# Time mix of an RWKV-style block: roots ahead of the mix's low halves, rows split ahead of the mix, the time row in the last bank, the first input in four transfers

## The reference, cut to what matters

```python
xn  = _layernorm(x)                       # the input of both branches
x1  = _ln(xn, ln1_g, ln1_b)
xln = _ln(x1, tm_g, tm_b)
xs  = _shift(xln)                         # one step later in time
mix = xln * time_first + xs * (1.0 - time_first)
v   = xln @ Wv
r   = sigmoid(mix @ Wr)
vmix = einsum('bth,th->bh', v, exp(time_decay * (T - 1 - t)))
x2  = xn + r * (vmix @ Wo + bo)
xc  = _ln(_ln(x2, ln2_g, ln2_b), cm_g, cm_b)
rc  = sigmoid(xc @ Wcr)                   # used later with relu(shift(xc) @ Wck)^2 @ Wcv
```

## Time and profile before

| | us |
|---|---|
| median of 3 runs | 1819.31 (1818.61 to 1824.56) |
| the profiled execution | 1819.79 |
| its span | 1818.2 |
| PE busy | 1671.1 (92%) |
| DVE busy | 1156.1 (64%) |
| ACT busy | 1032.1 (57%) |
| POOL busy | 507.7 (28%) |
| granted PE clock, mean | 0.98 |

### The profile page before, as it was taken

The page is one execution under the profiler, slowest core; times in us unless marked ns, Lnnn a source line. Parts: engine busy times, 40 slices in busy tenths (PEclk is TensorE's granted clock), DMA queues, the critical chain, the costliest instruction groups (busy, mean ns, idle before and its releaser), DMA issues.

```text
span 1818.2 us, 27152 instructions
## 1 busy us (share of the span) xinstructions
PE 1671.1 (92%) x9270; PEld 1424.0 (78%) x9270; DVE 1156.1 (64%) x2177; ACT 1032.1 (57%) x1809; POOL 507.7 (28%) x648
## 2 busy tenths in 40 slices
PE   2888899999999989999988999999999999999996
PEld 2666687877777777777776788989898898989895
DVE  6688632246787677687666776575666666666653
ACT  5466463334666666666764534565656565665652
POOL 3344310101122111222112031333334343433432
PEclk9899999999999999999999999999999999999998
DMA  5355657883356444575426445686767676767671
GB/s 193 115 169 189 194 181 197 249 238 91 104 171 140 113 130 120 136 202 131 110 79 170 108 152 188 211 276 204 265 214 254 227 246 227 251 226 259 223 245 24
DMA packets 114567, 328.21 MB, mean 181 GB/s; under 512 B 29615, under 2 KB 29615, under 8 KB 100722
## 3 DMA queue, kind: packets, MB, share of 16 engines
q1 hardware_dynamic: 94194, 287.42, 48.0%
q0 software_dynamic: 15696, 31.21, 9.5%
q10 hardware_dynamic: 4592, 8.52, 1.3%
HBM read 264.31 MB, written 68.94 MB: 183 GB/s over the span
## 4 chain that ended last, share of the span: by engine, by line
PE 59%; DVE 7%; ACT 6%; issue 4%; POOL 1%; DMA 1%; ACTq 0%; DVEq 0%; POOLq 0%
PE bank L53 17%; PE bank L55 17%; PE bank L54 17%; PE bank L2172 2%; DVE hd_a L1955 1%; PE bank L2158 1%; PE bank L2203 1%; DVE hd_masked L2014 1%; PE bank L2200 1%; DVE ex_w_lo L2608 1%; PE bank L2202 1%; ACT hd_a_hi L1823 1%; ACT hd_relu L1803 1%; PE bank L2711 1%; DVE hd_p_lo L2021 1%
## 5 line engine op out<-in xcount | busy, mean ns | idle before, releaser
L2608 DVE TENSOR_TENSOR ex_w_lo<-ex_stage,ex_w_hi 128x1024 fp32r<-128x1024 f32 x207 | 248.6, 1236 | 171.6 <-ACT ex_w_hi L2518 166.8
L1726 POOL TENSOR_SCALAR_AFFINE_SELECT hd_p_full<-hd_p_full 128x128 f32<-128x128 f32 (+1 forms) x192 | 93.0, 493 | 437.3 <-ACT hd_p_full L1853 434.5
L2444 POOL TENSOR_TENSOR ex_a_lo<-ex_a,ex_a_hi 128x256 fp32r<-128x256 f32 x128 | 92.6, 746 | 293.2 <-ACT ex_a_hi L2540 293.0
L53 PE MATMUL bank<-ex_x_hi_a,ex_w_hi 128*128 128x256 f32 x512 | 145.1, 283 | 0.4 <-DVE ex_a L2646 0.3
L53 PE MATMUL bank<-ex_x_hi_b,ex_w_hi 128*128 128x256 f32 x512 | 144.7, 283 | 0.0
L55 PE MATMUL bank<-ex_x_hi_b,ex_w_lo 128*128 128x256 f32 x512 | 144.3, 282 | 0.0
L54 PE MATMUL bank<-ex_x_lo_b,ex_w_hi 128*128 128x256 f32 x512 | 144.3, 282 | 0.0
L55 PE MATMUL bank<-ex_x_hi_a,ex_w_lo 128*128 128x256 f32 x512 | 144.2, 282 | 0.0
L54 PE MATMUL bank<-ex_x_lo_a,ex_w_hi 128*128 128x256 f32 x512 | 144.0, 281 | 0.0
L2515 ACT ACTIVATE ex_w_hi<-ex_stage 128x1024 fp32r<-128x1024 f32 x134 | 133.8, 1048 | 0.6 <-DMA ex_stage<-in_w_moe 0.6
L53 PE MATMUL bank<-ex_w_hi,ex_a_hi 128*128 128x512 f32 x312 | 126.2, 404 | 0.3 <-DVE ex_w_lo L2608 0.3
(11 more groups left out here) (321 smaller groups left out, 5000.9 us busy)
## 6 DMA issues: line engine op xcount, KB each, us to landing
ex_stage<-in_w_moe SPq DMA_DIRECT2D x69, 1536.0 KB, 6.9
first_w<-in_w_moe SPq DMA_DIRECT2D x23, 1536.0 KB, 6.8
st_qk<-scratch_qk SPq DMA_DIRECT2D x64, 256.0 KB, 3.7
st_raw<-in_w_up SPq DMA_DIRECT2D x64, 256.0 KB, 2.8
st_raw<-in_w_dn SPq DMA_DIRECT2D x64, 256.0 KB, 2.9
st_qk<-scratch_qk SPq DMA_DIRECT2D x128, 64.0 KB, 3.5
tm_x_in<-in_x SPq DMA_DIRECT2D x4, 1024.0 KB, 5.6
scratch_xn<-tm_xn SPq DMA_DIRECT2D x4, 1024.0 KB, 6.2
```

Of the source, the lines that this page charges most:

```text
L53: pe.matmul(out, lhsT=w_hi, rhs=x_hi, start=first, stop=False)
L1726: pool.affine_select(out=p_full[:, i % 2, at:at + blocks * P], in_=p_full[:, i % 2, at:at + blocks * P], compare_op=ALU.is_ge, fill=0.0, b ...
L2444: pool.tensor_tensor(a_lo[:, chunk.par, m, :], a[:, m, :], a_hi[:, chunk.par, m, :].bitcast(F32), ALU.subtract).then_inc(wide_lo_ready, 1)
L2608: return dve.tensor_tensor(dst, src, hi.bitcast(F32), ALU.subtract)
```

## The change

- POOL: the root for `x2(b)` and the roots for `x(b + 2)` now stand between `low_x(b + 1)` and `low_mix(b + 1)` of sequence b; `add_x2(b)` stands behind `low_mix(b + 1)`.
- `split_x`: ACT makes `xT` and `x_hi` of all four banks first (eight ops), and then the four parts of `mix` from `xT` in SBUF, with the scale `time_first` alone; the constants `tf_scale` fall away. `x_lo` waits for the two ops of its bank, `v` for two ops and one `x_lo` at a time, and frees bank m when it comes to it.
- `r` and `rc` wait for one low half at a time in their first row block (j = 0).
- The time row goes to bank 3; `turn_x(b + 1)` waits for the residual only ahead of its last bank. The same holds for `turn_xs(0)`.
- Start: `x_in` of batch 0 comes in four DMAs with a semaphore each, and the moments start on the first; the four centring ops stand ahead of the wait for the root; ACT makes `decay` ahead of `norm_x(0)`, splits weight 0 and 1 ahead of `norm_x1(0)`, each when its own DMA has landed, and weight 2 behind `high_mix(0)`; `inverse_roots_x(1)` follows `low_mix(0)` as before.

```diff
             def low_x(b):
-                low(x_lo, lambda c: xT[:, c, 1:S + 1], x_hi, x_split, b * 3 * HC, 3, x_lo_ready)
+                low(x_lo, lambda c: xT[:, c, 1:S + 1], x_hi, x_split, b * 3 * HC, 2, x_lo_ready)
...
-            def sequence(b, before, more):
-                if before:
-                    add_x2(b - 1)
-                    inverse_root(C, (b - 1) * STATS_C)
-                if more:
-                    inverse_roots_x(b + 1)
+            def sequence(b, before, more, more2):
                 if before:
                     inverse_root(C, (b - 1) * STATS_C + MOMENTS + AFFINE)
                 if more:
                     inverse_root(A, (b + 1) * STATS_A + FIRST + AFFINE)
-                if not more:
+                else:
                     root(0)
                 if before:
                     low_xc(b - 1, xcT)
                 if more:
                     low_x(b + 1)
+                inverse_root(C, b * STATS_C)
+                if more2:
+                    inverse_roots_x(b + 2)
+                if more:
                     low_mix(b + 1)
+                add_x2(b)
...
-                    act.activation(mix[:, c, :], psum[c][:, :], ACT.Identity, bias=tf_scale[:, 1, c:c + 1],
-                                   scale=tf_scale[:, 0, c:c + 1]).then_inc(x_split, 1)
+                act.wait_ge(x_split, b * 3 * HC + 2 * HC)
+                for c in range(HC):
+                    act.activation(mix[:, c, :], xT[:, c, 1:S + 1], ACT.Copy,
+                                   scale=vecs[:, V_TF, c:c + 1]).then_inc(x_split, 1)
...
-            norm_x(0)
             act.wait_ge(const_in, 16 * N_CONST)
...
+            norm_x(0, TT)
+            high_w(0)
+            high_w(1)
             norm_x1(0)
             act.wait_ge(consts_ready, CONSTS)
             split_x(0)
             high_mix(0)
+            high_w(2)
             sequence(0, False)
...
             first_moments_x(0, False)
-            first_scales_x(0)
             dve.wait_ge(const_in, 16 * N_CONST)
+            dve.wait_ge(stat[A], MOMENTS)
+            centred(A, t1, x_in, R_G1)
+            first_scales_x(0, TT)
...
-            norm_x1(0)
+            norm_x1(0, True)
...
-            def turn(src, bank, done):
+            def turn(src, bank, done, last_free=None):
                 for c in range(HC):
+                    if last_free and c == HC - 1:
+                        pe.wait_ge(*last_free)
...
                     for k in range(HC):
+                        if j == 0:
+                            pe.wait_ge(lo_ready, before + k + 1)
...
-                        if m == 0 and k == 0:
-                            pe.wait_ge(x_split, b * 3 * HC + 3 * HC)
+                        if k == 0:
+                            pe.wait_ge(x_split, b * 3 * HC + 2 * (m + 1))
...
-                    pe.matmul(psum[0][:, :], lhsT=vmix_wide[:, m, :], rhs=wo[:, m, :], start=(m == 0), stop=False)
+                    pe.matmul(psum[HC - 1][:, :], lhsT=vmix_wide[:, m, :], rhs=wo[:, m, :], start=(m == 0), stop=False)
...
-                pe.wait_ge(x2_step, b * 2 * TT + TT)
-                turn_x(b + 1)
+                turn_x(b + 1, True)
```

More of the change, by code:

```diff
@@ L153, in mix_project_phase @@
         const_in = sem("const_in")
-        w_in = sem("w_in")
+        w_in = [sem(f"w_in{n}") for n in range(3)]
         w_hi_ready = sem("w_hi_ready")
@@ L159, in mix_project_phase @@
         x_loaded = sem("x_loaded")
+        x0_loaded = [sem(f"x0_loaded{j}") for j in range(TT)]
         stat = {A: sem("stat_a"), C: sem("stat_c")}
@@ L211, in mix_project_phase @@
         N_CONST = 6
-        CONSTS = HC + 4
+        CONSTS = HC + 2
         R = TT + 1
@@ L247, in sequence @@
                     xc_halves_out(b - 1)
-            load_x(0)
+            for j in range(TT):
+                sp.dma_start(x_in[:, j, :], d["x"][0][j * P:(j + 1) * P, :]).then_inc(x0_loaded[j], 16)
             sp.dma_start(vecs[:, :, :], d["vecs"]).then_inc(const_in, 16)
@@ L409, in _ @@
             low_mix(0)
[L410 to L415, removed]
+            inverse_roots_x(1)
+            sequence(0, False, True, True)
+            with pool.Fori(1, B - 2) as b:
+                sequence(b, True, True, True)
+            sequence(B - 2, True, True, False)
+            sequence(B - 1, True, False, False)
             inverse_root(C, (B - 1) * STATS_C + MOMENTS + AFFINE)
@@ L432, in normed, with norm_x, high_w @@
                                    scale=rstd[:, chain, j:j + 1]).then_inc(ready, 1)
-            def norm_x(b):
-                normed(xn, x_in, A, b * STATS_A + FIRST, xn_ready)
+            def norm_x(b, first_halves=0):
+                normed(xn, x_in, A, b * STATS_A + FIRST + first_halves, xn_ready)
+            def high_w(n):
+                act.wait_ge(w_in[n], 16)
+                act.activation(w_hi[n][:, :, :].rearrange("p k n -> p (k n)"), w_stage[:, n, :],
+                               ACT.Copy).then_inc(w_hi_ready, 1)
             def norm_x1(b):
@@ L617, in scales, with centred @@
                 dve.wait_ge(stat[chain], end)
-            def affine_norm(chain, dst, src, row_g, row_b, at, root):
+            def centred(chain, dst, src, row_g):
                 for j in range(TT):
@@ L623, in affine_norm @@
                                              ALU.subtract, ALU.mult).then_inc(stat[chain], 1)
+            def affine_norm(chain, dst, src, row_g, row_b, at, root, begun=False):
+                if not begun:
+                    centred(chain, dst, src, row_g)
                 for j in range(TT):
@@ L801, in turn, with turn_x @@
                     t.then_inc(done, 1)
-            def turn_x(b):
+            def turn_x(b, before):
                 pe.wait_ge(norm_ready[A], b * TT + TT)
-                turn(t1, 0, x_turned)
+                turn(t1, 0, x_turned, (x2_step, (b - 1) * 2 * TT + TT) if before else None)
             def turn_xc(b):
@@ L833, in r @@
             def r(b):
-                pe.wait_ge(m_lo_ready, b * HC + HC)
-                by_token(1, m_hi, m_lo, r_done)
+                by_token(1, m_hi, m_lo, m_lo_ready, b * HC, r_done)
             def time_row(b):
@@ L840, in time_row @@
                 for m in range(HC):
[L841 to L842 removed]
+                    pe.matmul(psum[HC - 1][:, :], lhsT=vmix_wide[:, m, :], rhs=wo[:, m, :], start=(m == 0), stop=False)
+                pe.matmul(psum[HC - 1][:, :], lhsT=ones_row[:, :], rhs=bo_row[:, :], start=False,
                           stop=True).then_inc(r_done, 1)
             def rc(b):
[L846 to L847 removed]
+                by_token(2, xc_hi, xc_lo, xc_lo_ready, b * HC, rc_done)
             def sequence(b, before):
@@ L907, in _ @@
             pe.wait_ge(consts_ready, CONSTS)
-            turn_x(0)
+            turn_x(0, False)
             pe.wait_ge(w_lo_ready, 1)
```

38 lines of the change are left out of this document (15 added, 23 removed).

## The result

The changed kernel takes 1810.7 us (median of six runs, 1808.3 to 1816.9); the kernel before took 1824.4 in its six runs beside them (1818.6 to 1825.7). The ratio of the runs is 0.9941 with a 95% interval of 0.9925 to 0.9957: 10.8 us less (8 to 14), where 15.8 were forecast; the two medians lie 13.7 apart, at the edge of that interval. The sign is as forecast, the time is 0.7 outside the range. The profiled execution has a span of 1806.5 us instead of 1818.2.

What follows compares the result with a forecast made beforehand. TensorE was taken as the bound, its first-phase waits reaching the total whole. Terms 4.8 + 5.6 + 0.3 + 1.2 + 4.2 - 0.3 = 15.8 us off 1819.8 gave 1804.0, median 1803.5; range 1800 to 1810.

Steps and rivals of the forecast that it cites:

- The bound: TensorE sets the pace from the second phase on, so time taken out of the first phase comes out of the total whole.
- The start: Rows in at 12.2, turn_x(0) at 25.5 instead of 28.0, low_w(2) ending at 41.5 instead of 42.4.
- one of my signs of being wrong: Listed: low_w(2) ending after 42.4, idle ahead of L841, clock 0.50 beyond v's first block, new wait ahead of q(0)/second phase.
- The term of 0.9: At the start, DVE's path to batch 1 gains 0.9 us through low_w(2) ending sooner.
- turn_x(1): Its start leads by 4.8 us: 3.66 from the time row in bank 3, 0.3 from gate_r, 0.9 from the start.
- v(1): Starts 3.65 us after turn_x(1) instead of 9.24, gaining 5.6, for a lead of 10.4.
- the rival that small gaps hold the clock down: TensorE, fed by low halves, misses full clock in v(0), v(1), rc(2): 29 us lost, 1833 in all; chance 0.03.
- Batch 1: Roots' new place avoids a stall; waits of 0.90 and 0.30 go, those of 7.04 stay; lead 11.9.
- rc(2): With one wait for each xc_lo, rc(2) ends 3.8 to 4.4 us sooner, taken as 4.2.
- v_tokens(0): Comes close to q_lo and may wait: -0.3 us.
- the first rival: Part of the gain only, DVE ruling the path (late rows, slower beside POOL): lead 10, 1809 us; chance 0.2.

Runs made afterwards that it cites:

- u_bank: Changed kernel with the time row in bank 0 and the residual wait ahead of all of turn_x(b+1) and turn_xs(0) again: second phase at 376.75, profiled run 1811.0 us.
- u_split: Changed kernel with split_x in its old order (x_lo after three ops, v after all twelve): second phase at 385.06, profiled run 1823.3 us.
- b1_ahead: Changed kernel with batch 1 taken ahead at the start (weight 2 split before split_x(0), POOL's roots before low_mix(0)): second phase at 376.97, profiled run 1814.7 us.
- apart: Changed kernel with one more POOL wait, so low_xc(2) starts only after DVE's residual(3): second phase at 371.93, profiled run 1809.2 us.
- u_start: Changed kernel with its start set back (one load of x, nmr ahead of centring, three weights split before norm_x1(0)): second phase at 378.59, profiled run 1818.9 us.
- c_after: The changed kernel itself, run and profiled again: median 1813.3 us, ratio 0.9946 to the kernel before, second phase at 376.77.
- u_halves: Changed kernel with r and rc waiting for all four low halves again: second phase at 374.57, profiled run 1813.5 us.
- wv_ahead: Changed kernel with high_wp(2) moved ahead of norm_x2(3) on ACT: second phase at 369.82, profiled run 1808.9 us.

## Why the prediction was wrong, point by point

- **The bound** was right: TensorE's waits of the first phase set the time, and what is won there reaches the end: 11.2 us at the second phase, 11.7 in the span.
- **The start:** the step held in kind and not in size. The rows landed at 13.3, not 12.2, so turn_x(0) came at 26.7 and not at 25.5; in the other profiles with this start it came between 25.5 and 26.7, so the forecast is one end of what it does. low_w(2) ended at 42.9 instead of 41.5, 0.5 beyond the later of my bounds (42.4): it started 1.0 later than forecast and took 3.00 beside POOL. That was one of my signs of being wrong. The term of 0.9 measured 0.2 (`nmr` at 61.13 against 61.33), and undoing it cost nothing at turn_x(1). The four loads brought the start of the last statistic to 8.09 against about 10.0 before, and DVE then idled 3.84 us for the rows, as forecast. The Trainium skill's rule to join small transfers (DMA: Bandwidth & Descriptors, Rules for kernel authors) did not bear on this load: the last of the four had landed by 8.1, where the single one did.
- **turn_x(1):** the size of the term was right (4.05 of 4.8), its cause half of the truth. I put 3.66 down to the bank of the time row; with bank 0 the turn starts as soon (u_bank). The earlier v(0), which I had written off as not kept, also ends the time row and the residual in time. Without it the bank does most of what I said (u_split: turn_x(1) at 65.33, its last bank at 68.03). Each of the two edits removes the wait.
- **v(1)** started 4.1 behind turn_x(1) instead of 3.65, as each step took a little longer: the first bank 1.15, ACT's two ops 1.52, `x_lo` 1.41. Forecast lead 10.4, measured 9.2. The clock was at its full level in all of v(1), its matmuls 0.23 to 0.34 apart within each three (the half clock behind the wait of 5.21 fell into the transposes: 0.50 from 64.31 to 67); the rival that small gaps hold the clock down is refuted at v(0), v(1) and rc(2), where gaps of 0.2 to 0.7 left it at 1.00. The effect reported by the Trainium skill (TensorE: Matmul & The Clock Gate, A second HAM failure mode: psum-queue depth-cycling) showed in none of these stretches.
- **Batch 1:** right. The waits of 0.90 and 0.30 went, but for 0.20, the two of 7.04 stayed, and without the roots' new place 4.35 of wait and some 6 us at v_tokens(0) came back (I had said that the lead would shrink from 11.9 to about 5).
- **rc(2):** its lead grew by 5.1, forecast 4.2 with up to 1.5 more if the store of rc came sooner. The copy behind that store lies at 187.63, 12.3 sooner than before, where TensorE's lead is 10.8.
- **v_tokens(0), the step that failed.** I gave it 0.3. The lead fell from 15.9 to 11.4 there, nearly all in idle time, and by 1.5 more in clock, of which 1.3 came back later. The mechanism (it comes close to `q_lo` and may wait) was named; its price was wrong, for two reasons.
  - DVE's ops keep their duration only if POOL is idle. My sum moved the blocks of DVE and POOL against each other and kept the length of each as in the kernel before. From the start of residual(3) to the `nmr` of `t2` DVE took 26.81 instead of 24.14, 2.7 more, and the adds alone took 3.1 more. The row that would have told it was there: low_w(2) took 3.38 beside POOL and half of 4.49 alone. I used it as a bound for this one op and for no other.
  - `q_lo` hangs on DVE's chain from residual(3), whose lead is 10.8, and not on rc(2), whose lead I had let grow to 16.1. With the adds as long as before, `nmr` would have come at 221.4 and v_tokens(0) at about 229.5, a lead of 14.1 (an estimate from the rows: the way from `nmr` to v_tokens(0) is 8.07). So some 1.8 of the 4.5 would have been lost without the collision, and 2.7 are the collision's. The undoing of the halves agrees: rc(2) 5.3 later at its end moved v_tokens(0) by 0.7.
- **The size** of the first rival (a lead of about 10 us, by DVE slowed beside POOL) is what came out, at a chance of 0.2, but at another place than I gave it; that the number fits is luck. The range went to 1810.0, which takes in its 1809 and next to nothing for the spread of the runs: the kernel before ran from 1818.6 to 1828.1, and identical copies differ by 3 us at the second phase's start and by 6 in its length (1432.6 and 1438.3). Against the six runs of before that stood beside the changed kernel, the forecast of 15.8 would have been 1808.6. That belongs into a range as much as the unknown terms.

## What to carry to other kernels

When a change shifts two engines against each other, check each pair of ops that newly overlap, not only each wait: DVE ops with two inputs in SBUF took up to 2.7 times as long beside POOL's two-input ops. Follow a forecast lead to the next few joins behind the last edit, for there it is lost, and look for idle time of the feeding engine in which the late step could be done: one moved call on ACT brought TensorE to turn_xs(2) 3.5 to 4.4 us sooner in two pairs of profiles, though in the whole time it is 2.5 us with intervals that overlap. A cause read from a wait's last releaser ("the residual") may vanish by itself when everything ahead of it moves; undo it alone before crediting it. And where two edits can each remove the same wait, undoing one of them shows nothing of its worth; undo the other as well.

## What the runs showed of the hardware

DVE beside POOL, all ops over 128 x 512 float32, four of them, in the changed kernel unless named: adds of two SBUF operands 2.49 with POOL idle, 3.56 in part beside it, 6.14 (b1_ahead) and 6.68 beside POOL's subtractions from end to end. BATCH_NORM_STATS2, with one input, 2.47 beside the same POOL ops (from 66.24 to 68.7, POOL at `x_lo` from 66.98). POOL's four subtractions took 5.00 beside mostly one-input ops of DVE (apart) and 6.34 beside DVE's adds. The rows that show it, DVE and POOL in batch 3 of the changed kernel:

```profile
167.27 5.80 DVE L629 SCALAR_TENSOR_TENSOR tm_t<-tm_x,tm_mv,tm_rows 128x512 f32<-128x512 f32 x4
172.99 2.73 DVE L638 SCALAR_TENSOR_TENSOR tm_t<-tm_t,tm_rstd,tm_rows 128x512 f32<-128x512 f32 x4
```

```profile
165.52 6.33 POOL L367 TENSOR_TENSOR tm_m_lo<-tm_mix,tm_m_hi 128x512 fp32r<-128x512 f32 x4 [0.62 <-ACT tm_m_hi L473]
```

The same form of op takes 5.80 beside POOL and 2.73 right after it. The Trainium skill (GPSIMD Engine Reference, Specifications) says that GpSimd shares its SBUF interfaces with VectorE, and that they contend when a VectorE instruction has two SBUF inputs. The trace agrees, with 2.1 to 2.7 times the duration.

TensorE's clock ahead of turn_xs(2), by the wait there: behind 2.08 (u_start), 2.10 (u_split) and 1.89 (c_after) came a stretch at reduced granted clock (0.69 over the first 2.9 us in c_after), and the way to the second phase took 84.67. Behind 0.78 (the changed kernel), 1.88 (u_halves) and 2.04 (wv_ahead) the clock stayed at 1.00, and the way took 82.7 to 83.1. So the length of the idle time alone does not decide it, and nothing here shows what does:

```profile
292.10 2.66 PE L887 MATMUL bank<-ident,pj_xs 128*128 128x128 f32 x16 [1.89 <-ACT pj_xs L518]
```

```profile
291.56 1.97 PE L886 MATMUL bank<-ident,pj_xs 128*128 128x128 f32 x16 [1.88 <-ACT pj_xs L518]
```

The first is c_after, the second u_halves. TensorE fed by halves in gaps of 0.7, idle for 2.2 of 5 us, kept 1.00 (rc(2) of the changed kernel).
